# State sums by fp32 transposes, hidden variance root and projection copies on ScalarE, transposition in the tile's own turn, two tail turns fewer

## The reference

```python
xn = layernorm(x)
# attn: Mamba
x_ssm, x_gate = split(xn @ W_in + b_in)
x_conv = silu(causal_depthwise_conv(x_ssm, conv_w) + conv_b)      # 4 taps
B, C = split(x_conv @ W_bc + b_bc)                                # 16 states each
dt = softplus(x_conv @ W_dt + b_dt)
h[n] = h[n] * exp(dt * A[n]) + dt * x_conv * B[n]                 # scan along time, n of 16
y = sum_n h[n] * C[n] + x_conv * D
m = layernorm((y * silu(x_gate)) @ W_out + b_out + xn) * ln_g + ln_b
# ffn: top 2 of 8 experts
h = gelu(layernorm(xn @ w1[e] + b1[e]) * ln1_g + ln1_b)           # 256 -> 512
f = layernorm(sum_e weight_e * (h @ w2[e] + b2[e]) + xn) * ln_g + ln_b
out = x + m + f
```

## Time and profile before

| | |
|---|---|
| time, median of 3 runs | 2136.91 us (2131.9 to 2138.22) |
| profiled execution | 2137.39 us, span 2135.6 us |
| VectorE busy | 1866.7 us, 87% |
| TensorE busy | 1636.0 us, 77% |
| ScalarE busy | 1309.9 us, 61% |
| GpSimd busy | 1066.6 us, 50% |
| mean granted clock of TensorE | 0.905 of 2.4 GHz |

### The profile page before, as it was taken

One profiled execution on the slowest core, in us unless ns is written; L12 is line 12 of the kernel. 1 busy time (PEld: TensorE's weight loads), 2 busy tenths in 40 slices (PEclk: granted clock), 3 DMA queues, 4 the chain that ended last, 5 costly groups with the idle time before them and its releaser, 6 DMA issues. The chain is left out here.

```text
span 2135.6 us, 27505 instructions
## 1 busy us (share of the span) xinstructions
PE 1636.0 (77%) x5288; PEld 862.2 (40%) x5289; DVE 1866.7 (87%) x2815; ACT 1309.9 (61%) x2119; POOL 1066.6 (50%) x885
## 2 busy tenths in 40 slices
PE   4673899999999999999999999999999998300000
PEld 4551445454444444454444444454444545100000
DVE  6766799899989999898989889899989994399999
ACT  3431576767767676776767676767676673333333
POOL 3777444444444444444444444444444441477775
PEclk9996899999999999999999999999999999755555
DMA  7945222222222222222222222212222221344443
GB/s 210 340 161 211 69 76 70 85 79 72 77 74 75 88 75 70 84 71 79 75 69 79 84 74 79 77 62 89 74 74 79 72 77 58 103 141 149 154 149 120
DMA packets 144220, 213.93 MB, mean 100 GB/s; under 512 B 26470, under 2 KB 112358, under 8 KB 144121
## 3 DMA queue, kind: packets, MB, share of 16 engines
q1 hardware_dynamic: 126988, 170.96, 24.6%
q0 software_dynamic: 12288, 33.57, 4.7%
q10 hardware_dynamic: 4848, 8.56, 1.2%
HBM read 148.21 MB, written 64.82 MB: 100 GB/s over the span
## 5 line engine op out<-in xcount | busy, mean ns | idle before, releaser
L481 POOL TENSOR_TENSOR area<-area,more 128x1024 f32<-128x1024 f32 x258 | 608.0, 2357 | 700.2 <-DVE area L1059 700.2
L593 ACT ACTIVATE area<-area,A_sb 128x512 f32<-128x512 f32 x516 | 343.7, 714 | 271.3 <-DVE area L1059 271.0
L824 PE MATMUL psY<-area,ident 128*128 128x512 f32 x1032 | 490.4, 620 | 0.0
L1059 DVE TENSOR_TENSOR_SCAN area<-area 128x512 f32<-128x512 f32 x256 | 326.1, 1334 | 48.8 <-ACT area L593 17.8
L1059 DVE TENSOR_TENSOR_SCAN area<-area,h_last 128x512 f32<-128x512 f32 x256 | 345.4, 1408 | 14.0 <-PE psY L824 13.7
L1075 DVE TENSOR_TENSOR area<-area,psC 128x1024 f32<-128x1024 f32 x256 | 308.4, 1205 | 16.7 <-DVE hstats L1080 13.7
L797 PE MATMUL psH<-w_sb,ffn_xT 128*128 x556 | 267.9, 604 | 39.4 <-DVE h_norm L1089 34.4
L824 PEld LDWEIGHTS psY<-area,ident 128*128 128x128 f32 x1032 | 197.0, 200 | 209.5 <-issue 209.5
L807 PE MATMUL psX<-w_sb,h_T 128*128 x1024 | 256.1, 393 | 1.5 <-issue 1.5
L615 ACT ACTIVATE h_T<-psT,be_T,g_T 128x128 f32<-128x128 f32 x552 | 207.9, 457 | 6.2 <-issue 4.6
L807 PEld LDWEIGHTS psX<-w_sb,h_T 128*128 128x128 f32 x1024 | 184.7, 190 | 51.4 <-issue 31.3
(11 more groups left out here) (176 smaller groups left out, 2394.7 us busy)
## 6 DMA issues: line engine op xcount, KB each, us to landing
more<-B_rows_d SPq DMA_DIRECT2D x130, 512.0 KB, 3.8
xin<-sorted_x SPq DMA_DIRECT2D x140, 128.0 KB, 2.0
sorted_y<-y_out SPq DMA_DIRECT2D x138, 128.0 KB, 1.9
area<-xnT_d SPq DMA_DIRECT2D x18, 512.0 KB
mamba_d<-mo_stage SPq DMA_DIRECT2D x17, 512.0 KB, 2.8
area<-L_attn_x SPq DMA_DIRECT2D x8, 1024.0 KB, 6.1
xnT_d<-w_sb ACTq DMA_DIRECT2D x16, 512.0 KB, 3.3
w_sb<-L_ffn_w SPq DMA_DIRECT2D x16, 512.0 KB
```

Source lines behind the costliest of these rows:

```text
L481: pool.tensor_tensor(inflow[:, k], dtx, B_rep[par][:, k].rearrange("p (a t) -> p a t", a=1).to_broadcast([P, KD, CHUNK]), ALU.mult).then_i ...
L593: e = nc.scalar.activation(decay[:, k, hd], dt_sb[par][:, hd], ACT.Exp, scale=A_sb[:, hd, n:n + 1])
L824: m = nc.tensor.matmul(psY[:, hd * CHUNK:(hd + 1) * CHUNK], ident[:, :], h_sb[:, 2 * before + k, hd], start=False, stop=True, skip_group_c ...
L1059: a = V.tensor_tensor_scan(h_sb[:, buf, hd], decay[:, k, hd], inflow[:, k, hd], start, ALU.mult, ALU.add)
```

## The change

- `add_up` adds the states by 16 fp32 transposes of 128x128 (`is_transpose=True`, `start=False`) instead of 4 matmuls of 512 columns, so the sum stands transposed in `psY`. `seed` writes transposed too, in 8 matmuls of 128 columns. Once a chunk ScalarE copies the sum to SBUF (`copy_sum`) and TensorE turns it back (`transpose_sum`).
- The root of the hidden variance is Ln and Exp on ScalarE (`hidden_root`), GpSimd's two steps are gone, and its two inflow products follow each other directly. VectorE aggregates the statistics at once, after a small memset (`hold`).
- All takes from `psB` and two of the five steps of the split of B and C are ScalarE's. Two preloads per turn set the activation tables.
- `transpose_h(u)` waits for the normalisation of tile u itself. `down` follows one turn behind, with two buffers of `h_T`, into the other half of `psX`. `copy_xT` now waits for `up` and `down` of the turn before, and `transpose_x` for the copies.
- The tail has 8 turns, and ScalarE copies two tiles more behind it.

The diff of ScalarE and GpSimd, cut:

```diff
+AHEAD = 1
-FFN_TURNS = SORTED + LAG
+FFN_TURNS = SORTED
...
-            def rstd_of(u):
-                pool.wait_ge(S["var_ready"], u + 1)
-                pool.tensor_tensor(hve[:, :], hmv[:, 1:2], eps_col[:, :], ALU.add).then_inc(S["ve_h"], 1)
-                pool.wait_ge(S["ve_h"], u + 1)
-                pool.tensor_tensor(hrs[:, :], hve[:, :], half_neg[:, :], ALU.pow).then_inc(S["rstd_ready"], 1)
             for k in range(2):
...
             def copy_xT(t):
                 act.wait_ge(S["xin_T"], t + 1)
+                if isinstance(t, int) and t == 0:
+                    act.wait_ge(S["y_ready"], 1)
+                else:
+                    act.wait_ge(S["y_ready"], t)
+                    act.wait_ge(S["h_ready"], t)
                 nc.scalar.activation(ffn_xT[:, :, :], psX[:, 0:KD * P].rearrange("p (k t) -> p k t", k=KD), ACT.Copy
...
+            def hidden_root(u):
+                act.wait_ge(S["var_ready"], u + 1)
+                nc.scalar.activation(hln[:, :], hmv[:, 1:2], ACT.Ln, bias=eps_col[:, 0:1]).then_inc(S["hln_ready"], 1)
+                act.wait_ge(S["hln_ready"], u + 1)
+                nc.scalar.activation(hrs[:, :], hln[:, :], ACT.Exp, scale=-0.5).then_inc(S["rstd_ready"], 1)
...
+            def take(name, g, par):
+                hd = int(name[-1]) if name[-1].isdigit() else 0
+                if name[:3] == "ssm":
+                    act.wait_ge(S["ssm_ready"], 2 * g + hd + 1)
+                    act.wait_ge(S["xpad_free"], g + 1)
+                    nc.scalar.activation(xpad[:, hd, TAPS - 1:], psB[:, :], ACT.Identity, bias=b_in_sb[:, hd:hd + 1]
+                                         ).then_inc(S["xpad_ready"], 1)
...
+                elif name == "bc":
+                    if not isinstance(g, int):
+                        act.wait_ge(S["B_stored"], 16 * g)
+                    act.wait_ge(S["bc_ready"], g + 1)
+                    nc.scalar.activation(bc_f, psB[0:PARTS * BC, :], ACT.Identity, bias=b_bc_sb[:, 0:1])
+                    nc.scalar.activation(bc_parts[par], psB[0:PARTS * BC, :], ACT.Identity, bias=b_bc_sb[:, 0:1]
+                                         ).then_inc(S["bc_taken"], 1)
+                elif name[:2] == "dt":
...
+            def copy_sum(c):
+                act.wait_ge(S["sum_done"], c * PAIRS + 2)
+                nc.scalar.activation(y_sb[:, :, :], psY[:, :].rearrange("p (q d) -> p q d", q=TPC), ACT.Copy
+                                     ).then_inc(S["y_taken"], 1)
...
-                        if TASKS[pr - 1] in ("dt0", "dt1"):
-                            take_dt(int(TASKS[pr - 1][-1]), g, ahead)
+                        if pr == 0:
+                            copy_sum(c)
+                        if pr > 0 and TASKS[pr - 1] is not None:
+                            take(TASKS[pr - 1], g, ahead)
                         decay_of(s + 2, state[0], 0, g, par)
-                        copy_y(u)
                         decay_of(s + 3, state[1], 1, g, par)
+                        hidden_root(u)
                         copy_xT(u + 1)
+                        if pr == TASKS.index("bc") + 1:
+                            bc_middle(g, ahead)
                         if pr == DT_TAKEN:
                             soft_exp(g)
                             soft_ln(g)
-                        gelu(u, e)
+                        with_gelu()
+                        copy_y(u)
+                        gelu(u, pr % 2, e)
                         if pr == CONV_TURN:
                             act.wait_ge(S["seed_done"], g + 1)
                             conv_silu(g)
                         if pr == GATE_TURN:
                             gate_silu_of(c, half)
```

The diff of TensorE and VectorE, cut:

```diff
             def transpose_x(t):
                 pe.wait_ge(S["xin_loaded"], 16 * (t + 1))
+                if not (isinstance(t, int) and t == 0):
+                    pe.wait_ge(S["xT_copied"], t)
+                if not (isinstance(t, int) and t < 2):
+                    pe.wait_ge(S["y_copied"], t - 1)
...
             def transpose_h(u):
-                pe.wait_ge(S["norm_done"], u + 1)
+                pe.wait_ge(S["norm_done"], u + 1 + 1)
                 pe.wait_ge(S["gelu_done"], u + 1)
...
-            def down(u, e, dst=psX):
-                pe.wait_ge(S["xT_copied"], u + 1)
-                pe.wait_ge(S["gelu_done"], u + 1)
+            def down(u, buf, e):
+                pe.wait_ge(S["y_copied"], u + 1 + 1)
+                pe.wait_ge(S["gelu_done"], u + 1 + 1)
...
-            def add_up(u, before):
-                pe.wait_ge(S["hC_done"], 2 * u + 2)
+            def add_up(u, buf):
                 for k in range(2):
+                    pe.wait_ge(S["hC_done"], 2 * u + k + 1 + 2)
                     for hd in range(KD):
-                        m = nc.tensor.matmul(psY[:, hd * CHUNK:(hd + 1) * CHUNK], ident[:, :], h_sb[:, 2 * before + k, hd],
-                                             start=False, stop=True, skip_group_check=True)
+                        for q in range(TPC):
+                            m = nc.tensor.matmul(psY[:, q * DIM + hd * P:q * DIM + (hd + 1) * P],
+                                                 h_sb[:, 2 * buf + k, hd, q * P:(q + 1) * P], ident[:, :],
+                                                 is_transpose=True, start=False, stop=True, skip_group_check=True)
                 m.then_inc(S["sum_done"], 1)
-            def seed():
+            def seed(c):
+                if c is not None:
+                    pe.wait_ge(S["mo_copied"], c + 1)
+                for q in range(TPC):
+                    for hd in range(KD):
+                        m = nc.tensor.matmul(psY[:, q * DIM + hd * P:q * DIM + (hd + 1) * P], x_conv[:, hd, q * P:(q + 1) * P],
+                                             diagD[:, hd, :], start=(q * DIM % CHUNK == 0 and hd == 0), stop=True,
+                                             skip_group_check=True)
+                m.then_inc(S["seed_done"], 1)
+            def transpose_sum(c):
+                pe.wait_ge(S["y_taken"], c + 1)
                 for hd in range(KD):
-                    m = nc.tensor.matmul(psY[:, hd * CHUNK:(hd + 1) * CHUNK], diagD[:, hd, :], x_conv[:, hd], start=True, stop=True)
-                m.then_inc(S["seed_done"], 1)
+                    for q in range(TPC):
+                        m = nc.tensor.transpose(psY[:, hd * CHUNK + q * P:hd * CHUNK + (q + 1) * P],
+                                                y_sb[:, q, hd * P:(hd + 1) * P], ident[:, :])
+                m.then_inc(S["yT_ready"], 1)
...
                         par = half if pr < PAIRS - 1 else ahead
-                        e_down, e_up = expert(u - LAG), expert(u + 1)
-                        down(u, e_down)
+                        e_down, e_up = expert(u - 1), expert(u + 1)
                         transpose_h(u)
-                        spread_C(s + 1, pr * 2 + 1, 1, half, g)
-                        pe.wait_ge(S["y_copied"], u + 1)
-                        transpose_x(u + 1)
-                        if pr == 1:
-                            pe.wait_ge(S["mo_copied"], c + 1)
-                            seed()
-                        add_up(u, 1 - pr % 2)
-                        spread_C(s + 2, state[0], 0, par, g)
+                        up(u + 1, e_up)
+                        if pr == 0:
+                            for k in range(2):
+                                spread_C(s + 2 + k, state[k], k, par, g)
+                            project_out(c)
+                        if pr == PAIRS - 1:
+                            add_up(u, pr % 2)
                         if TASKS[pr] is not None:
                             wait_taken(TASKS[pr - 1] if pr else "gate1", g if pr else c)
                             task(TASKS[pr], g)
                         if pr == 0:
-                            project_out(c)
-                        up(u + 1, e_up)
-            add_up(MAMBA_TURNS, 1)
+                            seed(c)
+                        else:
+                            for k in range(2):
+                                spread_C(s + 2 + k, state[k], k, par, g)
+                        transpose_x(u + 2)
+                        if pr == PAIRS - 1:
+                            transpose_sum(c + 1)
+                        down(u - 1, (pr + 1) % 2, e_down)
+                        if pr != PAIRS - 1:
+                            add_up(u, pr % 2)
             project_out(CHUNKS)
...
-                down(u, e_down, dst=psC)
-                up(u + 1, e_up)
+            with pe.Fori(0, (FFN_TURNS - MAMBA_TURNS) // 2) as j:
+                for k in range(2):
+                    u = MAMBA_TURNS + j * 2 + k
+                    e_down, e_up = expert(u - 1), expert(u + 1)
+                    transpose_h(u)
+                    up(u + 1, e_up)
+                    transpose_x(u + 2)
+                    down(u - 1, 1 - k, e_down)
+            down(FFN_TURNS - 1, 1, expert(FFN_TURNS - 1))
...
```

(16 more changed lines are left out.)

169 lines of the change are left out of this document (85 added, 84 removed).

## The result

The changed kernel takes 2116.13 us in the median of 5 runs (2112.45 to 2120.63), the kernel before 2136.91 (2131.9 to 2140.21). The ratio is 0.9906, 95% interval 0.989 to 0.9922. So it is faster, by 0.94% where 3.5% was forecast, and 2116 us lies in the range.

What follows compares the result with a forecast made beforehand. VectorE and TensorE, busy 88.6 and 91.0 of 96.5 us a chunk, were taken as the bound. Stage minus 82.0, start minus 3 and tail plus 10.6 us took 2137.4 to 2063 us, range 2005 to 2137.

Steps and rivals of the forecast that it cites:

- Stage 16 x 91.5: Mamba stage: 16 chunks of 91.5 us each against 96.5, giving 1461.4 us for the stage against 1543.4.
- costs nothing: VectorE's subtraction `bc_residue`: taking 1.76 us instead of 0.7 adds no time, as ScalarE sets that turn.
- Turn 0 to 1: First turn of a chunk: base 8.7, gate 1.2, `copy_mo` 1.2 and the pad, 11.2 us in all.
- Turn 1 to 2: Second turn of a chunk: 13.5 us, with VectorE waiting 1.7 for the adding up and ScalarE's root at 24.7.
- The wait of that scan: Sign in turn 2: scans wait for the adding up of turn 0, which ends at 16.6 us; VectorE waits 1.7.
- the other sign: Sign in turns 4 and 5: `h_norm` on VectorE waits for ScalarE.
- The last interval: Turn 7 to 0: transposes, up and adding up 5.3, sum copy 1.1, decays 2.6, root 0.5, 9.5 us in all.
- cost like matmuls: Rival: adding transposes take 7.2 us a turn for 1.8, TensorE 122 us a chunk, about 2550 us; chance 4%.
- Tail turns: Tail behind the stage: 7.2 us a turn against 5.25 before, as `copy_xT` waits for `down` of the turn before.
- the rival's share: Clock rival: TensorE at half speed for f = 0.5 of the time, 105 us a chunk, 2284 us; chance 8%.
- waits pile up: Rival: waits in seven chains of three engines make a chunk 95 us, 2119 us in all; 20% for 2090 to 2143.
- TensorE's gain: Adding up by transposes on TensorE: 1.8 us less a turn, 14 a chunk; its 91.0 us become about 79.

Runs made afterwards that it cites:

- experiment 2: The changed kernel with TensorE's loop over single chunks instead of two chunks a pass; ratio 0.9724 to the kernel before, about 2078 us.
- experiment 9: The changed kernel with TensorE's 8 passes written out, with no loop and no branch; ratio 0.9715 to the kernel before.
- Experiment 11: The changed kernel with TensorE's loop over single chunks and VectorE's subtraction `bc_residue` moved behind the products with C; ratio 0.9649 to the kernel before.
- experiment 4: The changed kernel with seed and adding up by matmuls of 512 columns again, without the sum's copy and its transposes; ratio 0.9637, 2059 us.
- experiment 6: The changed kernel with wide adding up, and the root of the variance back on GpSimd in turns and tail; ratio 0.9797 to the kernel before.
- experiment 7: The changed kernel with wide adding up, and four takes a chunk (inner and gate halves) back on VectorE; ratio 1.0287 to the kernel before.

## Why the prediction was right in direction and wrong in size

In the balance of the two profiled spans the start gave 8.9 us (forecast 3; why more was not looked into), the stage 25.4 (forecast 82.0), and the rest took 10.2 (forecast 10.6).

**The step that failed** is "Stage 16 x 91.5": the cost of one chunk held for all. It was near 91.4 in every second chunk and 96.6 to 100.3 in the others, 94.9 on the mean. I had priced TensorE's instructions by their time in the array alone, and not by their number: 364 records more in a pass, for which the sum has no term. They cost the jump back, put at nothing: 3.4 to 4.7 us in each of 7 passes. The seven first turns behind a jump take 34 us more than seven others, of 13.05. Experiments 2 and 9 take the jump to lost instructions away and little else, and give 42.6 and 36.0 us of the 56.6 that were missing; the 6.6 between them go at least in part with the half-clock stretch in the fifth turn, which experiment 9 keeps. Experiment 11 gives 9.8 more: the prediction said of the subtraction that a longer one "costs nothing", which is true only where ScalarE sets the turn by enough. Together the stage is 1465.6, forecast 1461.4.

**The walk through a turn.** Medians of the second chunks, with the forecast (no clock, no last column) in brackets: 13.05 (11.2), 11.3 (13.5), 12.1 (11.6), 11.6 (11.05), 10.0 (10.2), 9.7 (9.3), 12.7 (12.8), 11.0 (9.5). The sum of 91.4 was met partly by luck. Turn 0 to 1 was forecast 1.9 too short: ScalarE's take waits 4.4 us for the projection behind `project_out`, the root stands behind that take, and VectorE waits 1.8 us for the root.

```profile
1090.73 0.69 ACT L634 ACTIVATE more<-psB,b_in_sb 128x512 f32<-128x512 f32 x1 [4.42 <-PE psB L919]
...
1094.31 0.81 DVE L1184 TENSOR_SCALAR h_norm<-psH,hmv,hrs 128x512 f32<-128x512 f32 x1 [1.82 <-ACT hrs L612]
```

Turn 1 to 2 was forecast 2.2 too long, and mostly for the same reason: it was worked out as 24.7 us for both turns less 11.2 for the first, and both turns together took 24.4. The seed was mis-sized besides, 16 records in 1.95 us and not 3.2, so the adding up of turn 0 ends at 15.2 us instead of 16.6, and VectorE comes to its scan 1.4 us later than that. The wait of that scan, which the prediction names as a sign, did not occur; VectorE itself sets the turn. Nor did the other sign: `h_norm` of turns 4 and 5 does not wait for ScalarE in this chunk. VectorE waits for ScalarE's steps of the split of B and C instead, 1.3 us ahead of `h_norm` of turn 4 and 0.6 behind it. The last interval lacked 1.5; in experiment 4, without the sum's copy and its transposes, it is 9.8.

**Terms that held.** Adding up: 16 records in 1.97 us (1.8 forecast), so the rival "cost like matmuls" is refuted. Busy in a second chunk: TensorE 80.1 (79), ScalarE 76.4 (77.5), VectorE 82.5 (near 80). The root in 0.28 to 0.29 and 0.20 us:

```profile
1047.26 0.29 ACT L610 ACTIVATE hln<-hmv,eps_col 128x1 f32<-128x1 f32 x1
1047.58 0.20 ACT L612 ACTIVATE hrs<-hln 128x1 f32<-128x1 f32 x1
1047.74 0.38 ACT L595 ACTIVATE ffn_xT<-psX 128x256 f32<-128x256 f32 x1
1048.14 1.28 ACT L626 ACT_TABLE_LOAD   x1
```

The gaps before and behind table loads stayed at 0.02 us or so, as in the earlier trace rows: the load at 982.31 us lasts 1.28, and `copy_y` starts at 983.61. The drain that the Trainium skill (ScalarE: Activation LUTs, "What ACT_TABLE_LOAD costs") adds was not there. Tail turns took 6.85 us (7.2), and the way from the last gate product to the end's first load 67.2 (68.1):

```profile
1792.79 0.81 DVE L1184 TENSOR_SCALAR h_norm<-psH,hmv,hrs 128x512 f32<-128x512 f32 x1 [2.28 <-ACT hrs L612]
...
1799.66 0.81 DVE L1184 TENSOR_SCALAR h_norm<-psH,hmv,hrs 128x512 f32<-128x512 f32 x1 [2.28 <-ACT hrs L612]
...
1809.26 0.35 SPq L404 DMA_DIRECT2D more<-L_attn_ln_g  x1
```

**The rivals.** The clock did not fall to the rival's share: 0.93 and 0.96 were granted. The time lies where "waits pile up" put it, but by another mechanism, since the chains' errors cancelled; that 2116 us fell into the range at all is luck. What the prediction took for TensorE's gain, 14 us of adding up a chunk, was off the path: with a short body and transposes the stage is 1475.4 (experiment 2), with a short body and wide matmuls 1456.0 (experiment 4). That experiment 4's 2059 us are close to the forecast's 2063 is luck as well: it is another kernel. By experiments 6 and 7 the root is worth 2.7 us a chunk and the takes, in this order, 8.5. What the order alone brings was not tried.

## What to carry to other kernels

Count the instructions in a loop's body, not only their time: a transformation into many small ones can push the body out of the engine's instruction store, and then each jump back costs what a fetch takes, here 3 to 5 us on the path. Look for "issue" waits at the top of a loop and for a queue of kind "instruction" that grew. Making an engine's work shorter gains nothing if it is not on the path: here the kernel with 8.5 us more of TensorE work in a chunk was the faster one.
